# State-space stage: y gathered by turning h, a step later; GpSimd multiplies quarters by C; the residual is added on TensorE; ScalarE's small work in a new order

## The chip, the cores and the metric

One core of a Trainium2 chip runs the whole kernel. The metric is device time in microseconds, the median of several runs. A core has five engines with instruction queues of their own that run in order: TensorE (PE in the profile; its weight loads are PEld), VectorE (DVE), ScalarE (ACT), GpSimd (POOL) and SyncE (SP, here only DMA issues). They wait for each other by semaphores.

## The reference, cut to what matters

A state-space layer of width 512 with 16 states on 2 sequences of 2048 tokens, then attention, then a mixture of experts. Only the first is touched:

```
xz = norm(x) @ W_in.T;  x_ssm, z = split(xz)
xc = silu(causal_conv4(x_ssm) + conv_b)
dt_raw, B, C = split(xc @ W_x.T)                      # 1, 16, 16 columns
dt = softplus(dt_raw * dt_w + dt_b)
h[t, d, n] = exp(dt * A[d, n]) * h[t-1, d, n] + dt * xc * B[t, n]
y[t, d]    = sum_n h[t, d, n] * C[t, n] + xc * D
x1 = x + (y * silu(z)) @ W_out.T
```

## The kernel before, in words

The stage cuts the tokens into chunks of 512 (CH), 4 in each of 2 sequences, and goes through them in turn, c = 2i + b, 8 chunks. Channels lie on the partitions: 512 channels are KI = 4 "quarters" of 128. A chunk is 16 steps, one for each state n. In a step:

- GpSimd makes bx = u * B_n, 128x2048 (L391), up to four steps ahead (ring of 4). The row of B comes by a broadcast DMA (`load_b`, L271).
- ScalarE makes dA = exp(dt * A), one 128x512 quarter at a time (L606), into two PSUM banks. A quarter can be written when the scan two quarters back is over.
- VectorE scans four quarters (L767) into h[n % 4]. Between the second and the third it multiplies the state of the step before by C (L774, 128x2048), where C_n was spread over the partitions by TensorE (`spread_c`, L652) into the single bank `c_ps`.
- ScalarE copies the last column of each scan into `state` (L499) before that multiplication.
- TensorE adds h*C into y_ps (4 banks, channels on the partitions) by a product with the identity (`collect`, L673, four products, eight records). At step n it does first `side`, then waits for the multiplication of state n - 1, spreads C_n, and collects n - 1. The scans of step n wait for the collect of n - 4.

The work of neighbouring chunks is hidden in these steps: `side` on TensorE, `side` and `between` on ScalarE (`between` stands ahead of the exponential of quarter 2, `side` after that of quarter 3), and the `if n == ...` lines on GpSimd. It is the input projection (L626), convolution (L634), the rows of dt, B and C (L642, L648), softplus (L475 to L495), the normalisation of the chunk after next (GpSimd, L343), silu of xc and z, and the output projection of the chunk before (L659), whose result VectorE adds to the residual (L758). The gate y * silu(z) is on VectorE in step 1 (L781). All of TensorE's small products go through one PSUM bank, `fill`, which is handed back and forth by the counts `s_full` and `s_free`. The order of its users is written out by hand as `fill_T`, `fill_E` and so on.

`prologue` does the first chunk's work and most of the second's ahead of the first scan; after the last scan come the gate, the output projection and the store of the last chunk.

The loop that couples ScalarE to VectorE:

```python
for d in range(KI):
    m = ND * c + KI * n + d
    if d == 2:
        if n > 0 or has_prev:
            save_state(*((c, b, n - 1) if n > 0 else (c - 1, 1 - b, NS - 1)))
        between(i, b, n, has_next)
    wait(act, s_scan, m - 1)
    nc.scalar.activation(dA[:, d % 2, :], dt[:, b, d, :], ACT.Exp, ...).then_inc(s_da, 1)
side(i, b, n, has_next)
```

## Time and profile before

| | |
|---|---|
| median of 3 runs | 3388.3 us (3386.0 to 3394.4) |
| profiled execution, its own time | 3382.5 us |
| its span, first to last instruction | 3381.1 us |
| mean granted TensorE clock | 0.934 of full |
| busy over the whole span | PE 2905.4, DVE 2411.4, ACT 1905.4, POOL 1090.3 us |
| broadcast of a row of B (L271), issue to landing | 3.1 us median of 128 |
| state-space stage: first scan / last store issued | 112.5 / 1081.0 us |

The page gives totals over stages with different limits, so the stage is read from queries with a window. "Timeline" lists instructions in order of time, neighbours of one line merged with their count; in brackets stands the idle time before them and who ended it. "Groups" are all instructions of one line and form. "Waits" sum the idle time of an engine by the instruction that waited and the one that released it. TensorE's fp32 product of 512 columns shows as two records.

### The profile page before, as it was taken

The numbers are of one execution on the slowest core, as the hardware profiler recorded it, in microseconds if no ns is written. First come the engines' busy times: TensorE is split into PE (matmuls) and PEld (weight loads), VectorE is DVE, ScalarE is ACT, GpSimd is POOL, SyncE is SP. The second block draws the span as 40 slices with busy tenths as digits, with TensorE's granted clock in tenths as the row PEclk, the third lists the DMA queues.
The fourth block names the chain that finished last, engine by engine and source line by source line (L and its number), as shares of the span: only waits on it lengthen the run. The fifth ranks groups of instructions, "written<-read, shape, count | busy, mean of one in ns | idle before, by whom it ended". The sixth has DMA issues, their size and how long they took to land. (4 is left out here: it accounts for less than half of the span.)

```text
span 3381.1 us, 45342 instructions
## 1 busy us (share of the span) xinstructions
PE 2905.4 (86%) x12880; PEld 1119.3 (33%) x12881; DVE 2411.4 (71%) x2674; ACT 1905.4 (56%) x3514; POOL 1090.3 (32%) x652
## 2 busy tenths in 40 slices
PE   5798899889775949999999999999999872999990
PEld 1234334334332512222222222222222262666650
DVE  0699999999996758888888888888888273111113
ACT  3556655665542517777777777777777611222320
POOL 2889778878862530000000000000000045000006
PEclk8999999999998969999999999999999975999995
DMA  1111111111111531111111111111110045111114
GB/s 42 41 50 48 41 57 55 39 48 49 41 48 39 183 94 32 38 39 39 39 39 39 38 34 36 37 39 39 39 39 10 30 144 201 46 45 45 45 37 146
DMA packets 123093, 185.25 MB, mean 55 GB/s; under 512 B 30224, under 2 KB 77968, under 8 KB 122896
## 3 DMA queue, kind: packets, MB, share of 16 engines
q1 hardware_dynamic: 109072, 142.95, 14.9%
q0 software_dynamic: 13824, 39.86, 3.7%
q8 instruction: 101, 1.65, 0.2%
q14 instruction: 96, 0.79, 0.1%
HBM read 138.01 MB, written 44.43 MB: 54 GB/s over the span
## 5 line engine op out<-in xcount | busy, mean ns | idle before, releaser
L1514 DVE TENSOR_REDUCE nmh<-ring 128x2 f32<-128x1024 f32 x1024 | 1188.0, 1218 | 226.5 <-PE ring L1406 225.1
L1387 ACT ACTIVATE prob<-s_ps 128x512 f32<-128x512 f32 x2048 | 1058.6, 605 | 315.9 <-PE s_ps L1427 313.7
L767 DVE TENSOR_TENSOR_SCAN h<-dA,state,bx 128x512 f32<-128x512 f32 x512 | 618.6, 1268 | 116.1 <-ACT dA L606 115.5
L391 POOL TENSOR_TENSOR bx<-u,bb 128x2048 f32<-128x2048 f32 x128 | 578.9, 4527 | 194.1 <-DVE h L767 193.9
L1427 PE MATMUL s_ps<-qs,ks 98*128 98x512 bf16 x2048 | 598.9, 388 | 16.9 <-issue 13.5
L1439 PE MATMUL acc<-prob,vst 128*32 128x512 f32 x4096 | 550.2, 609 | 0.7 <-ACT prob L1387 0.7
L606 ACT ACTIVATE dA<-dt,aneg 128x512 f32<-128x512 f32 x512 | 348.9, 691 | 270.4 <-DVE h L767 270.3
L673 PE MATMUL y_ps<-h,ident 128*128 128x512 f32 x1024 | 482.6, 616 | 1.1 <-DVE h L774 1.1
L1406 PE MATMUL ring<-k,q 64*128 64x512 bf16 x2048 | 368.4, 396 | 43.4 <-DMA k<-parts 23.6
L1427 PEld LDWEIGHTS s_ps<-qs,ks 98*128 98x128 bf16 x2048 | 157.6, 97 | 516.5 <-ACT prob L1387 423.1
L774 DVE TENSOR_TENSOR h<-h,c_ps 128x2048 f32<-128x2048 f32 x128 | 290.2, 2267 | 4.5 <-PE c_ps L652 4.2
L2225 DVE TENSOR_TENSOR mid<-sl,c_ps 128x512 f32<-128x512 f32 x72 | 49.5, 688 | 325.3 <-ACT sl L2210 325.3
L673 PEld LDWEIGHTS y_ps<-h,ident 128*128 128x128 f32 x1024 | 204.0, 199 | 226.6 <-issue 218.8
L1329 POOL CAST nmr<-a_rowf 16x128 bf16<-16x128 f32 x32 | 8.9, 279 | 769.9 <-ACT a_rowf L1372 769.9
L1406 PEld LDWEIGHTS ring<-k,q 64*128 64x128 bf16 x2048 | 79.7, 94 | 483.5 <-DVE nmh L1514 273.8
L1339 POOL TENSOR_TENSOR att<-oraw,rec 128x256 f32 (+1 forms) x32 | 19.8, 619 | 634.0 <-DVE rec L1528 634.0
L626 PE MATMUL fill<-xT,w_in 128*128 128x512 f32 x256 | 131.9, 640 | 38.0 <-ACT zs L446 18.4
L2210 ACT ACTIVATE sl<-a_ps 128x512 f32<-128x512 f32 x72 | 43.0, 597 | 208.0 <-PE c_ps L2274 208.0
L2166 POOL DMA_DIRECT2D xt<-slots_in x72 | 38.8, 539 | 355.7 <-PE x_ps L2238 348.8
L2274 PE MATMUL a_ps<-w,m_xT 128*128 x288 | 137.4, 600 | 0.3 <-issue 0.3
L2259 PE MATMUL o_ps<-w,midT 128*128 x576 | 136.4, 380 | 0.8 <-ACT midT L2206 0.8
L2274 PE MATMUL c_ps<-w,m_xT 128*128 x288 | 135.7, 594 | 0.0
(221 smaller groups left out, 2563.8 us busy)
## 6 DMA issues: line engine op xcount, KB each, us to landing
bb<-b_rows SPq DMA_DIRECT2D x128, 256.0 KB, 3.1
q<-parts SPq DMA_DIRECT2D x256, 64.0 KB, 2.1
parts<-part POOLq DMA_DIRECT2D x48, 256.0 KB, 3.1
qs<-parts SPq DMA_DIRECT2D x192, 64.0 KB, 2.8
ks<-parts SPq DMA_DIRECT2D x192, 64.0 KB, 2.8
xt<-slots_in POOLq DMA_DIRECT2D x72, 128.0 KB, 2.3
slots_out<-yt SPq DMA_DIRECT2D x72, 128.0 KB, 1.7
k<-parts SPq DMA_DIRECT2D x256, 32.0 KB, 2.0
```

The costliest lines, as they stand in the source:

```text
L391: nc.gpsimd.tensor_tensor(bx[:, n % BR], u[:, b], bb[:, n % RB, None, :].to_broadcast([P, KI, CH]), ALU.mult).then_inc(s_bx, 1)
L606: nc.scalar.activation(dA[:, d % 2, :], dt[:, b, d, :], ACT.Exp, scale=aneg[:, d, n:n + 1]).then_inc(s_da, 1)
L673: last = nc.tensor.matmul(y_ps[:, d, :], ident[:, :], h[:, n % HR, d, :], start=False, stop=(n == NS - 1))
L767: nc.vector.tensor_tensor_scan(h[:, n % HR, d, :], dA[:, d % 2, :], bx[:, n % BR, d, :], state[:, b, n, d:d + 1], ALU.mult, ALU.add).then_ ...
L774: nc.vector.tensor_tensor(h[:, n % HR], h[:, n % HR], c_ps[:, None, :].to_broadcast([P, KI, CH]), ALU.mult).then_inc(s_hc, 1)
L1387: nc.scalar.activation(prob[:, k % PR, j, :], s_ps[:, tile % SR, :], ACT.Exp, scale=SC).then_inc(s_exp, 1)
L1406: ins = nc.tensor.matmul(ring[:, s, half, :], q4[r, slot, t * P:(t + 1) * P], k4[r, slot, s * CH:(s + 1) * CH], start=True, stop=True)
L1427: nc.tensor.matmul(s_ps[:, tile % SR, :], ks[:, par, hh, t * P:(t + 1) * P], qs[:, par, hh, j * CH:(j + 1) * CH], start=True, stop=True).t ...
L1439: last = nc.tensor.matmul(acc[32 * j:32 * j + 32, :], vst[:, par, t, v0:v0 + 32], prob[:, k % PR, j, :], start=(t == 0), stop=(t == KT - 1))
L1514: nc.vector.tensor_reduce(nmh[:, slot, t, 2 * s:2 * s + 2], ring[:, s, :, :], AX.X, ALU.max, negate=True).then_inc(s_free[s], 1)
L2259: last = nc.tensor.matmul(o_ps[:, q % 2, 0:DM], midT[:, q % 2, m, :], of_expert(w2, e_down, m), start=(m == 0), stop=(m == KF - 1))
L2274: last = nc.tensor.matmul(dst[:, q % 2, :], xT[:, q % 2, k, :], of_expert(w, e_up, k), start=(k == 0), stop=(k == KM - 1))
```

## The change

- **Turned y.** y_ps and zs now hold tokens on the partitions and channels along the bank. `collect` turns 16 blocks of 128x128 with TensorE's transpose (`is_transpose`) that adds to PSUM, and does so one step later (n - 2 instead of n - 1). z is projected in the same layout (`project_z`). The skip part is 16 products of 128 columns instead of 4 of 512, and stands in step 2 behind `spread_c`. After the gate the result is turned back (`gated`, 4 blocks for each quarter, copied by ScalarE in `take_g`), then projected.
- **Quarters by GpSimd.** For 8 of the 16 states (SHARED) VectorE multiplies three quarters by C and GpSimd the fourth, four steps later, with rows of C that come by DMA (`c_rows`, `load_c`, two buffers). `collect` waits for it before its last four turnings.
- **Residual.** TensorE adds x by a product with the identity in `project_out`; ScalarE copies the result out (`take_o`) instead of VectorE's addition.
- **Normalisation** goes from GpSimd to ScalarE (`normalize`, four instructions), with a small product on VectorE (`mean_part`).
- **Order.** ScalarE's small work has new places: softplus_in one quarter at a time, take_conv 3 in step 0, take_rows in step 2, z in steps 9 and 10, the chunk after next from step 11. TensorE's side work moves with it. VectorE's gate goes from the middle to the end of step 1.
- At the end the turning back uses four free banks (`end_banks`), each copied by ScalarE, and store_x1 moves from step 13 to 15.

```diff
+    RC = 2
+    SHARED = (0, 2, 10, 11, 12, 13, 14, 15)
+    NP = len(SHARED)
...
+        zs = sb("zs", [P, 2, TT, DI])
...
+        y_ps = ps("y_ps", [P, TT, DI])
...
+            def load_c(i, b, n):
+                c, k = 2 * i + b, SHARED.index(n)
+                wait_apart(sp, s_prst, 32 * (c + 1), s_w)
+                wait_apart(sp, s_hp, NP * c + k - RC + 1, s_w)
+                sp.dma_start(cc[:, k % RC, :], c_dram[b, n:n + 1, :].partition_broadcast(P)
+                             ).then_inc(s_c[k % RC], 16)
...
+                    if n - RC in SHARED:
+                        load_c(i, b, n - RC)
+                    elif n - RC + NS in SHARED and has_prev:
+                        load_c(*prv(i, b), n - RC + NS)
...
+            def times_c(c, n):
+                k = SHARED.index(n)
+                wait(pool, s_c[k % RC], 16 * ((NP // RC) * c + k // RC + 1))
+                wait(pool, s_sv, NS * c + n + 1)
+                nc.gpsimd.tensor_tensor(h[:, n % HR, KI - 1, :], h[:, n % HR, KI - 1, :], cc[:, k % RC, :], ALU.mult
+                                        ).then_inc(s_hp, 1)
...
+                    if n - BR in SHARED:
+                        times_c(c, n - BR)
+                    elif n - BR + NS in SHARED and has_prev:
+                        times_c(c - 1, n - BR + NS)
                     if n == 6 and has_next:
                         rest(c + 1, 1 - b)
-                    if n == 8 and has_two(i):
-                        norm_apply(c + 2)
-                    if n == 9 and has_next:
-                        rest_of_rest(c + 1)
                     if n == 10 and has_next:
                         rounding(c + 1)
                     if n == 11 and has_next:
+                        rest_of_rest(c + 1)
                         log_part(c + 1, 1 - b)
...
+            def normalize(c, t):
+                wait(act, s_mr, c + 1)
+                last = nc.scalar.activation(xn[:, t, :], xn[:, t, :], ACT.Identity, bias=mr[:, t:t + 1],
+                                            scale=rs[:, t:t + 1])
+                if t == TT - 1:
+                    last.then_inc(s_xn, 1)
...
+            def between(i, b, n, has_prev, has_next):
                 c = 2 * i + b
                 two = has_two(i)
-                if n == 1 and has_next:
-                    take_conv(c + 1, 1 - b, 3)
-                if n == 3 and has_next:
-                    take_rows(c + 1, 1 - b)
-                if n == 8 and has_next:
-                    take_z(c + 1, 1 - b, 1)
-                if n == 9 and has_next:
-                    take_z(c + 1, 1 - b, 3)
+                if has_next:
+                    if n in (3, 4):
+                        softplus_in(c + 1, 1 - b, 2 * n - 6)
+                    if n == 8:
+                        second_part(c + 1, 1 - b)
+                    if n in (9, 10):
+                        take_z(c + 1, 1 - b, 2 * n - 18)
+                if n in (6, 7) and has_prev:
+                    take_g(c - 1, 1 - b, 2 * n - 11)
                 if two:
-                    if n == 10:
-                        take_xT(c + 2, 1)
+                    if n in (6, 7):
+                        normalize(c + 2, n - 6)
+                    if n == 9:
+                        normalize(c + 2, 2)
+                        normalize(c + 2, 3)
                     if n == 11:
-                        take_conv_in(c + 2, 1)
+                        take_xT(c + 2, 0)
                     if n == 12:
-                        take_conv_in(c + 2, 3)
-                    if n in (13, 14, 15):
-                        take_conv(c + 2, b, n - 13)
-
-            def side(i, b, n, has_next):
+                        place_halo(c + 2, b)
+                    if n in (12, 13):
+                        take_conv_in(c + 2, 2 * n - 24)
+                    if n == 14:
+                        take_conv(c + 2, b, 0)
+
+            def side(i, b, n, has_prev, has_next):
                 c = 2 * i + b
                 two = has_two(i)
+                if n == 0 and has_next:
+                    take_conv(c + 1, 1 - b, 3)
                 if n == 1:
                     if has_next:
                         silu_xc(c + 1, 1 - b)
                     silu_z(c, b)
                     power_tables()
-                if n == 2 and two:
-                    root(c + 2)
-                if n == 3 and has_next:
-                    softplus_in(c + 1, 1 - b, 0)
-                if n == 4 and has_next:
-                    softplus_in(c + 1, 1 - b, 1)
-                if n == 5 and has_next:
-                    softplus_exp(c + 1)
-                if n == 6 and has_next:
-                    softplus_plus(c + 1)
-                    second_part(c + 1, 1 - b)
-                if n == 7 and has_next:
-                    softplus_minus(c + 1)
-                    take_z(c + 1, 1 - b, 0)
-                if n == 8 and has_next:
-                    softplus_ln(c + 1, 1 - b)
-                    take_z(c + 1, 1 - b, 2)
-                if n == 9:
+                if n == 2:
                     if has_next:
+                        take_rows(c + 1, 1 - b)
+                    if two:
+                        root(c + 2)
+                if n in (5, 6) and has_prev:
+                    take_g(c - 1, 1 - b, 2 * n - 10)
+                if n in (7, 8) and has_prev:
+                    take_o(c - 1, n - 7)
+                if has_next:
+                    if n in (3, 4):
+                        softplus_in(c + 1, 1 - b, 2 * n - 5)
+                    if n == 5:
+                        softplus_exp(c + 1)
+                    if n == 6:
+                        softplus_plus(c + 1)
+                    if n == 7:
+                        softplus_minus(c + 1)
+                    if n == 8:
+                        softplus_ln(c + 1, 1 - b)
+                    if n in (9, 10):
+                        take_z(c + 1, 1 - b, 2 * n - 17)
+                    if n == 14:
                         third_part(c + 1, 1 - b)
-                    if two:
-                        take_xT(c + 2, 0)
                 if two:
-                    if n == 10:
-                        place_halo(c + 2, b)
-                        take_conv_in(c + 2, 0)
                     if n == 11:
-                        take_conv_in(c + 2, 2)
+                        take_xT(c + 2, 1)
+                    if n in (12, 13):
+                        take_conv_in(c + 2, 2 * n - 23)
+                    if n in (14, 15):
+                        take_conv(c + 2, b, n - 13)
...
+            def project_z(c, t):
+                wait(pe, s_free, fill_Z(c, t))
+                for k in range(KM):
+                    last = nc.tensor.matmul(fill[:, :], xT[:, k, t * P:(t + 1) * P], w_in[:, k, DI:2 * DI],
+                                            start=(k == 0), stop=(k == KM - 1))
+                last.then_inc(s_full, 1)
+
+            def turn_back(bank, b, d):
+                for t in range(TT):
+                    last = nc.tensor.transpose(bank[:, t * P:(t + 1) * P], zs[:, b, t, d * P:(d + 1) * P], ident[:, :])
+                return last
+
+            def gated(c, b, d):
...
             def project_out(c, b, half):
                 wait(pe, s_free, fill_O(c, half))
+                wait(pe, s_xr, 16 * (c + 1))
                 for t in (2 * half, 2 * half + 1):
+                    nc.tensor.matmul(fill[:, (t % 2) * DM:(t % 2 + 1) * DM], ident[:, :], xres[:, t, :],
+                                     start=True, stop=False)
                     for d in range(KI):
                         last = nc.tensor.matmul(fill[:, (t % 2) * DM:(t % 2 + 1) * DM],
-                                                zs[:, b, d, t * P:(t + 1) * P], w_out[:, d, :],
-                                                start=(d == 0), stop=(d == KI - 1))
+                                                zs[:, b, t, d * P:(d + 1) * P], w_out[:, d, :],
+                                                start=False, stop=(d == KI - 1))
                 last.then_inc(s_full, 1)
             def skip_part(c, b):
                 wait(pe, s_g, c)
+                for t in range(TT):
+                    for d in range(KI):
...
                 for d in range(KI):
-                    last = nc.tensor.matmul(y_ps[:, d, :], diag[:, d, :], xc[:, b, d, :],
-                                            start=True, stop=False)
-                last.then_inc(s_dx, 1)
-
-            def collect(n):
-                for d in range(KI):
-                    last = nc.tensor.matmul(y_ps[:, d, :], ident[:, :], h[:, n % HR, d, :],
-                                            start=False, stop=(n == NS - 1))
+                    if n in SHARED and d == KI - 1:
+                        wait(pe, s_hp, NP * c + SHARED.index(n) + 1)
+                    for t in range(TT):
+                        last = nc.tensor.matmul(y_ps[:, t, d * P:(d + 1) * P], h[:, n % HR, d, t * P:(t + 1) * P],
+                                                ident[:, :], is_transpose=True, start=False,
+                                                stop=(n == NS - 1 and d == KI - 1))
                 last.then_inc(s_ys, 1)
             def prologue():
...
                 two = has_two(i)
-                if n == 0 and has_next:
-                    convolve(c + 1, 3)
-                if n == 1:
-                    skip_part(c, b)
-                if n == 2 and has_next:
-                    project_rows(c + 1, 1 - b)
-                if n == 3 and has_next:
-                    spread_dt(c + 1)
-                if n in (5, 6) and has_prev:
-                    project_out(c - 1, 1 - b, n - 5)
-                if n in (7, 8) and has_next:
-                    project_in(c + 1, KI + 2 * n - 14)
-                    project_in(c + 1, KI + 2 * n - 13)
+                if has_next:
+                    if n == 0:
+                        convolve(c + 1, 3)
+                    if n == 2:
+                        project_rows(c + 1, 1 - b)
+                    if n == 3:
+                        spread_dt(c + 1)
+                if has_prev:
+                    if n in (5, 6):
+                        gated(c - 1, 1 - b, 2 * n - 10)
+                        gated(c - 1, 1 - b, 2 * n - 9)
+                    if n in (7, 8):
+                        project_out(c - 1, 1 - b, n - 7)
+                if has_next:
+                    if n == 8:
+                        project_z(c + 1, 0)
+                    if n == 9:
+                        project_z(c + 1, 1)
+                        project_z(c + 1, 2)
+                    if n == 10:
+                        project_z(c + 1, 3)
                 if two:
-                    if n == 9:
-                        transposes(c + 2, 0)
-                        transposes(c + 2, 1)
                     if n in (10, 11):
-                        project_in(c + 2, 2 * n - 20)
-                        project_in(c + 2, 2 * n - 19)
-                    if n in (12, 13, 14):
-                        convolve(c + 2, n - 12)
+                        transposes(c + 2, n - 10)
+                    if n == 11:
+                        project_in(c + 2, 0)
+                    if n == 12:
+                        project_in(c + 2, 1)
+                        project_in(c + 2, 2)
+                    if n == 13:
+                        project_in(c + 2, 3)
+                        convolve(c + 2, 0)
+                    if n in (14, 15):
+                        convolve(c + 2, n - 13)
             def chunk(i, b, has_prev, has_next):
                 c = 2 * i + b
...
-                        collect(NS - 1)
+                        collect(c - 1, n - 2 + NS)
             every_chunk(pe, prologue, chunk)
+            collect(NC - 1, NS - 2)
             wait(pe, s_hc, NS * NC)
-            collect(NS - 1)
...
-                                        c_ps[:, None, :].to_broadcast([P, KI, CH]), ALU.mult
+                mine = KI - 1 if n in SHARED else KI
+                nc.vector.tensor_tensor(h[:, n % HR, 0:mine], h[:, n % HR, 0:mine],
+                                        c_ps[:, None, :].to_broadcast([P, mine, CH]), ALU.mult
                                         ).then_inc(s_hc, 1)
...
-                    if n == 1 and has_prev:
-                        gate(c - 1, 1 - b)
                     if n > 0:
                         times_c(c, b, n - 1)
                     elif has_prev:
                         times_c(c - 1, 1 - b, NS - 1)
-                    if n in (6, 7) and has_prev:
-                        residual(c - 1, n - 6)
                     scans(c, b, n, 1)
                     if n == 1 and has_two(i):
                         norm_stats(c + 2)
+                    if n == 1 and has_prev:
+                        gate(c - 1, 1 - b)
+                    if n == 4 and has_two(i):
+                        mean_part(c + 2)
             every_chunk(dve, prologue, chunk)
             times_c(NC - 1, 1, NS - 1)
             gate(NC - 1, 1)
```

## Rows read from the trace of the kernel before

**Rows 1.** Windows, 500 to 600 us: length, PE, PEld, DVE, ACT, POOL, clock, DMA.
```profile
500.00:600.00 100.00, 90.14 (x224) 41.75 (x225) 96.74 (x71) 60.73 (x97) 84.09 (x23) 0.95 0.18 54
```

**Rows 2.** Groups by form, first 1300 us: count, busy us, mean ns, idle before.
```profile
L767 DVE TENSOR_TENSOR_SCAN h<-dA,state,bx 128x512 f32<-128x512 f32 x512 | 618.6, 1268 | 116.1 <-ACT dA L606 115.5 <-issue 0.6
L391 POOL TENSOR_TENSOR bx<-u,bb 128x2048 f32<-128x2048 f32 x128 | 578.9, 4527 | 194.1 <-DVE h L767 193.9
...
L774 DVE TENSOR_TENSOR h<-h,c_ps 128x2048 f32<-128x2048 f32 x128 | 290.2, 2267 | 4.5 <-PE c_ps L652 4.2 <-ACT state L499 0.3
...
L758 DVE TENSOR_TENSOR xres<-fill,xres 128x512 f32<-128x512 f32 x16 | 11.0, 690 | 9.5 <-PE fill L659 9.5
...
L1004 ACT COPY v_all<-v_ps 128x256 f32<-128x256 f32 x8 | 2.4, 387 | 0.1
```

**Rows 3.** Waits, first 1300 us: us in total, times, longest.
```profile
DVE h L767 <- ACT dA L606: 115.5, 27, 91.3
```

**Rows 4.** The scans' line by itself: min, median, max ns, first and last start.
```profile
L767 DVE TENSOR_TENSOR_SCAN h<-dA,state,bx x512: 1248/1265/1296, 112.5 to 1060.2; 128x512 f32<-128x512 f32 x171
```

**Rows 5.** Timeline of VectorE: start us, length us, what, count, idle before.
```profile
527.89 2.46 DVE L767 TENSOR_TENSOR_SCAN h<-dA,state,bx 128x512 f32<-128x512 f32 x2 [0.93 <-ACT dA L606]
...
547.37 4.80 DVE L767 TENSOR_TENSOR_SCAN h<-dA,state,bx 128x512 f32<-128x512 f32 x4
552.08 2.27 DVE L774 TENSOR_TENSOR h<-h,c_ps 128x2048 f32<-128x2048 f32 x1
554.26 2.45 DVE L767 TENSOR_TENSOR_SCAN h<-dA,state,bx 128x512 f32<-128x512 f32 x2
```

**Rows 6.** Timeline of ScalarE, same columns.
```profile
494.67 0.78 ACT L475 ACTIVATE xs<-fill,dtb,dtw 128x512 f32<-128x512 f32 x1 [1.09 <-PE fill L648]
...
496.01 0.78 ACT L475 ACTIVATE xs<-fill,dtb,dtw 128x512 f32<-128x512 f32 x1
...
522.48 1.99 ACT L492 ACTIVATE tB<-tB,minus 128x2048 f32<-128x2048 f32 x1
...
549.85 0.69 ACT L606 ACTIVATE dA<-dt,aneg 128x512 f32<-128x512 f32 x1 [0.48 <-DVE h L767]
...
550.81 0.59 ACT L434 COPY xs<-fill 128x512 f32<-128x512 f32 x1 [0.15 <-PE fill L626]
```

**Rows 7.** Timeline of TensorE's products in the stage.
```profile
493.51 1.12 PE L648 MATMUL fill<-pr,sel_f 17*128 17x512 f32 x2
...
509.14 3.62 PE L659 MATMUL fill<-w_out,zs 128*128 128x256 f32 x16
...
550.61 0.38 PE L652 MATMUL c_ps<-c_parts,sel 96*128 96x512 bf16 x1
550.83 3.60 PE L673 MATMUL y_ps<-h,ident 128*128 128x512 f32 x8
554.27 1.88 PE L626 MATMUL fill<-xT,w_in 128*128 128x512 f32 x4
...
562.30 3.60 PE L634 MATMUL fill<-xs,taps 128*128 128x512 f32 x8
```

**Rows 8.** Timeline of TensorE in the routing stage and the expert stage.
```profile
2709.57 1.95 PE L1889 MATMUL g_ps<-gate,gT 128*128 128x8 f32 x16 [1.36 <-ACT gT L1827]
...
2713.63 5.21 PE L1863 MATMUL h_ps<-wo,attT 128*128 128x256 f32 x16 [1.18 <-ACT attT L1815]
...
2902.40 0.60 PE L2266 MATMUL m_ps<-m_ident,mid 128*128 128x128 f32 x4
```

**Rows 9.** Timeline of TensorE, a skip part and a collect after idling.
```profile
237.80 5.40 PE L667 MATMUL y_ps<-xc,diag 128*128 128x512 f32 x8 [2.38 <-DVE zs L781]
...
263.44 0.61 PE L652 MATMUL c_ps<-c_parts,sel 96*128 96x512 bf16 x1 [4.12 <-DVE h L774]
263.84 6.33 PE L673 MATMUL y_ps<-h,ident 128*128 128x512 f32 x8
```

**Rows 10.** Timeline of GpSimd, the rounding.
```profile
524.59 4.16 POOL L358 TENSOR_TENSOR tB<-tB,xs 128x2048 f32<-128x2048 f32 x1
```

141 lines of the change are left out of this document (86 added, 55 removed).

## The prediction

> **What bounds the kernel now.** I read the page's 40 slices first: the state-space stage fills the first third of the span and is the only stage that the diff touches. Then the busy time of one hundred-microsecond stretch [rows 1]: VectorE 96.7, TensorE 90.1, GpSimd 84.1, ScalarE 60.7. VectorE leads, and its groups say with what [rows 2]: 512 scans and 128 multiplications by C. The waits [rows 3] tell how full it is: of 115.5 us of idling before scans, 91.3 is the one wait for the prologue, so only 24.2 us is lost after it. The scans run from 112.5 to 1060.2 plus one scan [rows 4], 949 us; 925 of them are work. So a microsecond less of VectorE work is a microsecond gained, as long as nobody else makes it wait.
>
> The timeline of VectorE gives a step [rows 5]: two scans, a multiplication, two scans; four scans are 4.71 (547.37 to 552.08), the multiplication 2.18 to the next start, a step 6.89. ScalarE is coupled to it through two dA banks [rows 6]. I set a step's clock to zero at its first scan. The exponential of quarter 1 runs from 0.1 to 0.8, then the state copy and whatever stands in `between`, from 0.83 on; then quarter 2; quarter 3 when scan 1 is over, 2.45 to 3.1; then whatever stands in `side`; the next step's quarter 0 must be ready at 6.89. So `between` must be over near 3.9 and `side` near 6.2. All of today's 24 us is ScalarE overrunning such a slot, as 0.93 in [rows 5].
>
> **VectorE's work.** A quarter of the multiplication: (2267 - 690) ns over 1536 elements is 1.03 ns an element [rows 2], 0.53 us for 512. 64 of 128 multiplications lose a quarter, 63 of them before the last scan: -33.2. A shortened step is 6.36. Residual: 14 of 16 lie before the last scan, 0.69 less the 0.09 by which neighbours overlap: -8.4. Six small `mean_part`, not in the trace, below 0.3 each and not below zero: +0.9 taken. The gate only moves. Sum -40.7.
>
> **GpSimd's work.** Eight products of 128x512, a quarter of 4.53 each [rows 2], +9.1 a chunk; normalisation -4.8. It has slack: 84 of 100 busy. All scans take 1248 to 1296 ns [rows 4] with GpSimd busy beside most of them, so I add nothing for the pair; 0 to 3 us as a bound.
>
> **SyncE's queue.** Eight more broadcast loads a chunk, as large as those of B, and a second store of rows. `load_c` waits for the product two before it and `load_b` stands behind it; but that wait ends right after bx n, and the load behind is for bx n + 4, some 20 us of GpSimd work on, where a load lands in half a step. Nothing added; if it did bind, GpSimd would come late in steps 14 to 2, where it has 5 us in hand.
>
> **TensorE's work.** [rows 7]: spreading C takes 0.22 to the next start, collecting 3.43, a projection 1.7 (ScalarE may read 1.91 after its start), a convolution 3.43 (3.63), half an output projection 3.5, dt 0.86 (1.16). A turning takes one record where a product takes two: four last 0.60 with 0.27 of it tail [rows 8], so 0.11 each, and a collect of sixteen is 1.75: -1.7 a step, if a turning that accumulates costs as much. Bounds 1.75 to 3.5 (two records each). The skip part becomes 32 records of 128 columns, each with a new weight load; 16 records of 8 columns with new weights take 1.95 [rows 8], under 0.12 each, so 3.5 to 3.9, about as now. Output projection: 20 records of 0.215 for 16, 4.3, ready 4.5. So TensorE gets lighter by about a fifth. It isn't the bound, though: what matters is when its results arrive, because ScalarE's queue is in order, and dA stands behind each wait.
>
> **Walking the new order, step by step.** A wait in ScalarE's `between` or `side` holds the dA queued behind it, and VectorE's scan behind that.
> - Step 3. In step 2 TensorE waits for multiplication 1 (ends 4.63), spreads C (0.22), then does the skip part (3.5), then collects (1.75): 10.2, which is 3.3 in step 3. Only then comes the dt row, ready at 4.4. ScalarE stands before it since 0.83, now in `between`, with quarter 2 behind. The Abs/Relu pair is 1.34 [rows 6], dA 0.62: 6.4, where the scan wants it at 4.0 (2.36 + 1.65). 2.4 lost, and the second pair in `side` 0.3 more: 2.7, in 7 chunks, 18.9. Today the wait is 1.09 in `side` and costs 0.67.
> - Step 7. The output projection can start when ScalarE has taken the last turned bank, 1.45, and is ready at 6.0. ScalarE, at `side` since 3.1, waits, copies (0.58), does the minus-one pass (1.9 in [rows 6]), then dA: 9.2 against 6.89, 2.3 lost in 6 chunks. In the last chunk, without that pass, 0.4.
> - Steps 12 to 14. GpSimd's rounding needs that late pass (8.6), a lag of over 3 on [rows 10], where it starts right after bx. Four more large operations of 4.2 to 4.5 stand among its bx, so the product for state 10, behind bx 14, is ready 46.5 after step 7's start. TensorE collects state 10 at step 12 and waits for it until 4.4 in step 13. Behind it stand a projection, ready 6.3 (wanted near 5.1: 1.2 lost), a convolution, C for step 13 (late, hidden), and in step 14 the convolution that ScalarE waits for until 8.4: 3.5 lost. 4.7 in each of 5 chunks, 2.2 in the first, which has no step-7 stall ahead: 25.7.
> - Elsewhere the slots hold: step 1's 6.5 us of silu and tables lies beside 1.86 of statistics and the gate, steps 9 to 12 have waits of 0.3 with room. +2 for these.
>
> **The clock.** After an idle of 4.12 the collect took 6.33, not 3.60; after 2.38 the skip part took 5.40, though its eight records are of the same size [rows 7, 9]. In the new order TensorE is idle for some 7 us into step 4, then has only turnings until step 7. So I let half of the output projection of step 7 run at 1.2 GHz: +2.3 in 7 chunks, 16, and a third of the 1.8 that the skip part lost there, +0.6 in 7, 4. Bounds: 0 and +4.3 for each output projection, 0 and 5.5 for each step 3.
>
> **What a page says against it.** In the routing stage, turnings and 8-column products fill much of the time, idles are only 1.2 to 1.4, and yet the product of 16 records takes 5.21 [rows 8] where 3.5 is the full-clock time [rows 7]: turnings seem to hold the clock poorly. The Trainium skill, "TensorE: Matmul & The Clock Gate", section "Part 4: PE-mode transpose", states that transposes do not count as busy for the clock gate in the way matmuls do. By that rule the third rival is what happens; without it the sum stands.
>
> **Ends.** Prologue: normalising goes from GpSimd to ScalarE, whose chain leads to the first scan: twice four of 0.39 [rows 2], +3.2, the GpSimd time saved hangs on nothing. Epilogue: four turned banks and their copies (about 3), 8 records more (2), less a quarter product and half a collect: +3.
>
> **Sum.** Idle within the stage 18.9 + 13.8 + 0.4 + 25.7 + 2 + 20 = 80.8 less today's 24.2: +56.6. Work -40.7. Ends +6.2. Total +22; against the profiled execution (span 3381.1, its own time 3382.5) 3404, and the median of the runs lies 5.8 above that execution: 3410.
>
> **Rivals.** (1) *The slots hold.* The stage still waits only about 24 us, because the dt row and the output projection are early enough: -40.7 + 6 = -35, 3353; with half the stalls walked, -7 to -18, 3370 to 3381. For it: VectorE is the fullest engine, TensorE gets lighter. Against: TensorE's order in steps 2 and 3. (2) *About equal*: the work saved and the stalls cancel within 10 us; that is the walk without the clock term, +2, 3390. (3) *The clock falls for good.* If turnings don't hold it, steps 9 to 12 run at 1.2 GHz too. Their products and turnings, 19 us at 2.4, become 38 in 27 us of steps: +11 in 6 chunks, 66, with the other terms 3470. It decides from the point where doubled work passes a step, 3.4 at full clock; steps 9 and 12 have 5.4. (4) *Accumulating turnings take two records*: 1.75 more a step, no relief; behind the late products of 12 to 14 this adds 3 to 4 a chunk, 3435.
>
> **Chances.** Forecast (stalls win, 3399 to 3430) 0.37; rival 1 0.28; rival 2 0.19; rival 3 0.11; rival 4 0.05. Over 0.3% faster, which is about what a measurement can tell: rival 1, 0.28; same 0.19; slower 0.53. The range reaches into rival 1 and up to the weaker forms of 3: 3352 to 3450; the likeliest case's own is 3399 to 3430.
>
> **What would show it.** Right: VectorE's idle before scans behind dA near 70 to 80 us after the first wait, the longest before quarter 2 of step 3 and quarter 0 of steps 8 and 15; ScalarE's waits for `fill` by the dt row and the output projection; TensorE waiting for GpSimd's h in step 12; collects of 1.75 to 3.5. The three-quarter multiplication at 1.74. Wrong: dt taken without a wait in step 3, a lighter TensorE that is early everywhere, or a clock that stays at 2.4 GHz through step 7.

## The result, and the profile after

| | before | after |
|---|---|---|
| median (8 runs each) | 3387.2 us (3382.4 to 3394.5) | 3401.15 us (3391.7 to 3407.0) |
| ratio of the medians, 95% interval | | 1.0040 (1.0028 to 1.0052) |
| profiled execution, its own time / its span | 3382.5 / 3381.1 us | 3403.2 / 3402.5 us |
| mean granted TensorE clock | 0.934 | 0.905 |
| first / last scan starts | 112.5 / 1060.2 us | 122.1 / 1075.1 us |

The changed kernel is 0.4% slower, 14 us by the medians, 21.4 by the two spans. The window of 500 to 600 us answers to [rows 1], columns as there:

```profile
500.00:600.00 100.00, 75.72 (x374) 53.72 (x373) 89.06 (x68) 63.77 (x109) 79.96 (x23) 0.91 0.17 56
```

VectorE had 96.7 us of work in it and now has 89.1; TensorE went from 90.1 to 75.7, though it issues more records. Work was taken away, and the time was not used. The groups by form, first 1300 us, answer to [rows 2]:

```profile
L875 DVE TENSOR_TENSOR_SCAN h<-dA,state,bx 128x512 f32<-128x512 f32 x512 | 618.8, 1263 | 112.4 <-ACT dA L668 111.7
...
L763 PE MATMUL y_ps<-ident,h 128*128 128x128 f32 x2048 | 314.6, 319 | 19.6 <-POOL h L398 19.6
...
L883 DVE TENSOR_TENSOR h<-h,c_ps 128x2048 f32<-128x2048 f32 x64 | 144.6, 2260 | 0.0
...
L883 DVE TENSOR_TENSOR h<-h,c_ps 128x1536 f32<-128x1536 f32 x64 | 110.7, 1730 | 6.2 <-PE c_ps L735 5.9 <-ACT state L546 0.3
L398 POOL TENSOR_TENSOR h<-h,cc 128x512 f32<-128x512 f32 x64 | 80.9, 1263 | 16.1 <-ACT state L546 16.1
```

64 multiplications now take 1.73 us instead of 2.26. The idle time before the scans is 111.7 us, nearly as before [rows 2, 3], but its make-up isn't: the first wait, for the prologue, is now 46.2, because an operation of VectorE in the prologue splits it, and what is left is 65.5 where it was 24.2.

The 21.4 us of the spans lie as follows. First scan 9.6 later. From the first to the last scan 953.0 instead of 947.7, +5.3. From the last scan to the issue of the last store 21.9 instead of 20.8, +1.1. From there to the end +5.4, in stages that are the same in both kernels. The +5.3 of the scans' stretch is the sum that matters. VectorE is busy for 877.0 us of it where it was busy for 917.5 before, so its work is 40.5 less and its idle time 45.9 more (76.0 against 30.1). Of the 76.0, 74.8 are waits on other engines: 65.5 for dA, 5.9 for c_ps, 3.1 for y_ps in two gates, 0.3 for the state.

### The profile page after: what moved, and what is told of

Same layout as the page of the kernel before. It is cut to its first block and busy times, and to the rows that moved or that the text cites. A ratio compares the mean times of both kernels' runs of the same rounds, so it can differ in the third digit from the quotient of the medians.

```text
span 3402.5 us, 48600 instructions
## 1 busy us (share of the span) xinstructions
PE 2797.3 (82%) x14288; PEld 1253.4 (37%) x14289; DVE 2370.1 (70%) x2666; ACT 1944.1 (57%) x3594; POOL 1131.7 (33%) x684
## 5 line engine op out<-in xcount | busy, mean ns | idle before, releaser
L875 DVE TENSOR_TENSOR_SCAN h<-dA,state,bx 128x512 f32<-128x512 f32 x512 | 618.8, 1263 | 112.4 <-ACT dA L668 111.7
L1515 PE MATMUL ring<-k,q 64*128 64x512 bf16 x2048 | 368.0, 396 | 43.6 <-DMA k<-parts 23.9
L763 PE MATMUL y_ps<-ident,h 128*128 128x128 f32 x2048 | 314.6, 319 | 19.6 <-POOL h L398 19.6
L763 PEld LDWEIGHTS y_ps<-ident,h 128*128 128x128 f32 x2048 | 296.8, 168 | 51.3 <-POOL h L398 22.9
L883 DVE TENSOR_TENSOR h<-h,c_ps 128x1536 f32<-128x1536 f32 (+1 forms) x128 | 255.3, 1995 | 6.2 <-PE c_ps L735 5.9
L735 PE MATMUL c_ps<-c_parts,sel 96*128 96x512 bf16 x128 | 58.8, 459 | 163.5 <-DVE h L883 163.1
```

The lines of the kernel that those rows point to most:

```text
L763: last = nc.tensor.matmul(y_ps[:, t, d * P:(d + 1) * P], h[:, n % HR, d, t * P:(t + 1) * P], ident[:, :], is_transpose=True, start=False, ...
L875: nc.vector.tensor_tensor_scan(h[:, n % HR, d, :], dA[:, d % 2, :], bx[:, n % BR, d, :], state[:, b, n, d:d + 1], ALU.mult, ALU.add).then_ ...
L883: nc.vector.tensor_tensor(h[:, n % HR, 0:mine], h[:, n % HR, 0:mine], c_ps[:, None, :].to_broadcast([P, mine, CH]), ALU.mult).then_inc(s_h ...
L1515: ins = nc.tensor.matmul(ring[:, s, half, :], q4[r, slot, t * P:(t + 1) * P], k4[r, slot, s * CH:(s + 1) * CH], start=True, stop=True)
```

## Where VectorE waits: one chunk of the kernel after

Three timelines of the chunk whose step 2 begins at 867, columns as in [rows 5]. VectorE, steps 2 to 4 and the end of step 7:

```profile
876.49 1.73 DVE L883 TENSOR_TENSOR h<-h,c_ps 128x1536 f32<-128x1536 f32 x1
880.77 2.46 DVE L875 TENSOR_TENSOR_SCAN h<-dA,state,bx 128x512 f32<-128x512 f32 x2 [2.55 <-ACT dA L668]
883.43 2.46 DVE L875 TENSOR_TENSOR_SCAN h<-dA,state,bx 128x512 f32<-128x512 f32 x2 [0.20 <-ACT dA L668]
...
913.43 2.46 DVE L875 TENSOR_TENSOR_SCAN h<-dA,state,bx 128x512 f32<-128x512 f32 x2 [2.30 <-ACT dA L668]
```

ScalarE in the same stretch:

```profile
878.71 0.78 ACT L522 ACTIVATE xs<-fill,dtb,dtw 128x512 f32<-128x512 f32 x1 [3.64 <-PE fill L731]
879.39 0.77 ACT L524 ACTIVATE dt<-fill,dtb,dtw 128x512 f32<-128x512 f32 x1
880.05 1.30 ACT L668 ACTIVATE dA<-dt,aneg 128x512 f32<-128x512 f32 x2
...
910.23 0.59 ACT L461 COPY xres<-fill 128x512 f32<-128x512 f32 x1 [2.92 <-PE fill L745]
910.71 2.01 ACT L539 ACTIVATE tB<-tB,minus 128x2048 f32<-128x2048 f32 x1
912.62 1.29 ACT L668 ACTIVATE dA<-dt,aneg 128x512 f32<-128x512 f32 x2
```

And TensorE:

```profile
871.91 0.39 PE L735 MATMUL c_ps<-c_parts,sel 96*128 96x512 bf16 x1 [2.45 <-DVE h L883]
872.14 3.74 PE L754 MATMUL y_ps<-diag,xc 128*128 128x128 f32 x32
875.71 1.91 PE L763 MATMUL y_ps<-ident,h 128*128 128x128 f32 x16
877.55 1.12 PE L731 MATMUL fill<-pr,sel_f 17*128 17x512 f32 x2
...
906.14 1.89 PE L745 MATMUL fill<-w_out,zs 128*128 128x256 f32 x8
907.87 0.59 PE L742 MATMUL fill<-xres,ident 128*128 128x256 f32 x2
908.30 1.89 PE L745 MATMUL fill<-w_out,zs 128*128 128x256 f32 x8
```

Read backwards: the scan at 880.77 waits 2.55 for an exponential at 880.05. That one stands behind the Abs/Relu pair at 878.71, which had waited 3.64 for the dt row at 877.55. And the dt row stands behind C, the skip part and a collect. In step 7 the same shape: the exponentials at 912.62 stand behind a pass of 2.01, that behind a copy that waited 2.92 for the output projection.

## The experiments

Each kernel was timed in rounds with the kernel before beside it. There are three groups of runs: e1 to e4 ("before" 3375.2 us), c1, e5, e6 and e7 (3376.5), e8 to e10 (3377.1, on another chip). A ratio is to the runs of "before" in the same group, and differs by up to 0.0011 from the quotient of the medians; its interval is 95%. On these chips the kernel before is some 10 us faster than in the table of the result, so medians are compared within this table alone. "Stretch" is the time from the start of the first scan to the start of the last, from the profile.

| kernel | median us | ratio | stretch | idle before scans for dA, first wait left out |
|---|---|---|---|---|
| c1_after | 3393.9 | 1.0050 (1.0037 to 1.0064) | 949.0 | 61.5 |
| e1_dt_early | 3372.0 | 0.9983 (0.9974 to 0.9992) | 935.8 | 41.0 |
| e2_minus_first | 3384.1 | 1.0019 (1.0008 to 1.0030) | 938.5 | 55.4 |
| e3_both | 3360.2 | 0.9948 (0.9934 to 0.9962) | 919.0 | 27.7 |
| e4_both_pool | 3351.2 | 0.9918 (0.9903 to 0.9932) | 919.5 | 28.1 |
| e5_twice | 3458.8 | 1.0238 (1.0223 to 1.0253) | 1018.4 | 124.0 |
| e6_ordinary | 3457.2 | 1.0234 (1.0219 to 1.0249) | 1018.1 | 123.8 |
| e7_noshare | 3399.3 | 1.0070 (1.0057 to 1.0083) | 958.8 | 45.4 |
| e8_mended | 3342.9 | 0.9896 (0.9882 to 0.9911) | 910.7 | 29.7 |
| e9_share10 | 3334.1 | 0.9876 (0.9862 to 0.9890) | 900.3 | 28.7 |
| e10_mended_noshare | 3356.2 | 0.9939 (0.9927 to 0.9951) | 924.9 | 13.7 |

**c1_after: the change itself, once more, beside the others.**

> The changed kernel itself, as the yardstick for the other three on this chip: 1.004 of the kernel before, first scan between 115 and 122 us depending on where TensorE's clock rises in the prologue.

1.0050 against 1.0040: the two agree within their intervals. Its scans began at 115.0, 7.1 us earlier than in the profile of after, and its stretch is 4.0 shorter: 1.3 us over the 947.7 of before, with 41.9 more idle and 40.6 less work. So VectorE gave back all of its saved work in both profiles, and 1 to 5 us more. That is also how far two profiles of the same code lie apart.

### Step 3: the dt row behind C, the skip part and a collect

**e1_dt_early** moves the two products of the dt row into step 2, behind `spread_c` and ahead of the skip part:

```diff
-                    if n == 3:
-                        spread_dt(c + 1)
...
+                        if has_next:
+                            spread_dt(c + 1)
                         skip_part(c, b)
```

> The changed kernel with one move: TensorE spreads the dt row in step 2, right behind spread_c, ahead of the skip part and the collect, instead of at the head of step 3. Theory A (the order of TensorE's queue makes the step-3 stall): VectorE's idle before the scan of quarter 2 in step 3, 26 us in 7 chunks in the changed kernel, goes to under 3; the rest stays; about 3401 - 22 = 3379. Rival B (the dt row is late because ScalarE's take_rows or the clock is late): the stall stays above 12 us and the time above 3390. Rival C (ScalarE is full anyway, the stall comes back in step 4 or 5): idle moves there, time within 5 us of the changed kernel.

22 us less than c1_after. The waits before scans in its stage:

```profile
DVE h L875 <- ACT dA L668: 82.0, 23, 41.0
...
DVE h L875 <- PE y_ps L763: 9.5, 6, 1.7
```

The idle for dA fell by 20.5 us and no scan of step 3 waits for it. But a new wait of 9.5 us came: with step 3 short, the scans of step 4 catch up with the collect that has to free their place in h, 1.4 to 1.7 us in each of six chunks. So the cause is shown, and the stall had covered a second one behind it. The stretch shows 13 us of the gain; the medians show 22, and where the other 9 lie the profiles don't say (the profiled execution of c1_after is 9.8 us below its median, that of e1 4.9).

### Steps 7 and 13 to 15: the minus-one pass behind the output projection

**e2_minus_first** puts `take_o(c - 1, 0)` behind the pass instead of ahead of it:

```diff
-                if n in (7, 8) and has_prev:
+                if n == 8 and has_prev:
                     take_o(c - 1, n - 7)
...
                     if n == 7:
                         softplus_minus(c + 1)
+                if n == 7 and has_prev:
+                    take_o(c - 1, 0)
```

> The changed kernel with one move: in ScalarE's step 7 the minus-one pass of softplus stands ahead of the copy of the output projection, not behind it. Both theories: VectorE's idle before step 8, 2.2 us in 6 chunks, goes to about 0.3 (-11), and GpSimd's wait for the pass before the rounding (23.9 us in 7) to about 0. Theory A (GpSimd's lag from that wait makes the stalls of steps 13 and 14): these fall from 4.6 to about 2.2 us a chunk, TensorE's wait for GpSimd's h in step 12 goes, and the time falls by 20 to 24, to 3379. Rival B (TensorE's own chain of projections and convolutions makes them): they stay at 4.6, the time falls by 11, to 3390.

9.8 us less than c1_after. By the time that is rival B's figure; the waits show that theory A's chain is there too. Step 7's wait shrank, and part of it came back one step later. The second scan here is the one that opens step 9:

```profile
890.48 2.46 DVE L878 TENSOR_TENSOR_SCAN h<-dA,state,bx 128x512 f32<-128x512 f32 x2 [0.41 <-ACT dA L671]
...
898.56 2.46 DVE L878 TENSOR_TENSOR_SCAN h<-dA,state,bx 128x512 f32<-128x512 f32 x2 [1.08 <-ACT dA L671]
```

ScalarE shows the same shape as in step 7, with the next pass of softplus behind the copy of the second half of the output projection:

```profile
895.45 0.59 ACT L461 COPY xres<-fill 128x512 f32<-128x512 f32 x1 [1.79 <-PE fill L748]
895.94 1.92 ACT L542 ACTIVATE u<-xs 128x2048 f32<-128x2048 f32 x1
```

GpSimd's wait for the pass fell from 23.9 us to 3.0 (seven times each), TensorE's wait for GpSimd's quarter from 18.5 in eleven times (c1_after) to 1.5 in three. The idle of steps 13 to 15 fell from about 4.5 to 1.95 us in three of the six chunks. The first, which has no output projection in step 7, stayed at 3.4, one stayed at 6.5, and one fell to 3.9. That it fell at all, though nothing was changed there, shows the chain: late pass, late rounding, late quarter, late collect, late projection, late dA. Against c1_after steps 7 and 8 idle 5 us less, steps 13 to 15 8 less, and step 3 idles 3 more, since the skip part took 4.86 and 5.01 in two chunks where c1_after has 3.74.

**e3_both** makes both edits.

> Both moves, dt row early and minus-one pass first. If the two stalls are independent the gains add: -42 to -46 against the changed kernel, 3357, which is 30 below the kernel before; VectorE's idle behind dA in the stage, 65 us in the changed kernel, near 20. If GpSimd or ScalarE becomes the bound once VectorE no longer waits, the sum is 10 us or more short of the two single gains.

33.7 us less than c1_after; the two alone give 21.9 and 9.8. The gains add, and more than add in the stretch (30.0, where the two alone give 13.2 and 10.5). It is short of the 42 to 46 expected because the second edit alone brought half of what had been expected of it. With two small products moved and one line put behind another the change is 0.5% faster than the kernel before.

**e4_both_pool** is e3_both with the prologue's two normalisations back on GpSimd (four `tensor_scalar` on `xn` for each of the first two chunks, as the kernel before does it):

```diff
+            def norm_apply(c):
+                wait_apart(pool, s_rs, c + 1, s_w)
+                for t in range(TT):
+                    last = nc.gpsimd.tensor_scalar(xn[:, t, :], xn[:, t, :], mv[:, t, 0:1], rs[:, t:t + 1],
+                                                   ALU.subtract, ALU.mult)
+                last.then_inc(s_xn, 1)
...
-                for t in range(TT):
-                    normalize(0, t)
...
-                for t in range(TT):
-                    normalize(1, t)
```

> As the last one, and in the prologue alone the two normalisations are again on GpSimd, as in the kernel before. The first scan came at 112.5 us before and at 122.1 after. Theory A (four ScalarE passes each time, and a stretch at 1.2 GHz that they lengthen): it comes at 112.5 to 114 again and the time falls by 8 to 10 more, to 3348. Rival B (the clock's phase at the start made half of it): only 4 to 5 come back.

9 us less by the medians. Its profiled execution, 3355.9 us, shows a part of it. Its first transpositions began at 13.05 instead of 15.38 in e3_both, and the projection ahead of which the second normalisation stood waits 5.97 instead of 7.93: 4.3 us gained by the move. But three projections more ran at 1.2 GHz there (3.78 us each, not 1.98), and two other products took 1.4 longer, so that the scans began at 117.6 against 115.1. The other 5 us of the medians this profile doesn't place.

### Do turnings hold TensorE's clock?

The pair **e5_twice** and **e6_ordinary** gives `collect` 32 records of the same size in both, once as turnings, once as ordinary products of two records each. e5 counts every h*C twice in y.

```diff
-                    for t in range(TT):
...
+                    for r in range(2):
+                        for t in range(TT):
+                            last = nc.tensor.matmul(y_ps[:, t, d * P:(d + 1) * P],
+                                                    h[:, n % HR, d, t * P:(t + 1) * P],
+                                                    ident[:, :], is_transpose=True, start=False,
+                                                    stop=(n == NS - 1 and d == KI - 1 and r == 1))
```

```diff
-                                                ident[:, :], is_transpose=True, start=False,
+                                                ident[:, :], start=False,
```

> The changed kernel, but collect turns each block twice (32 turnings instead of 16), so that y counts double: a test of the clock. In the last eight steps, where TensorE has nothing else, a step holds 3.7 us of turnings in 6.4 to 6.9 us, as much as the kernel before had of products, whose collects there took 3.6 us at 2.4 GHz. If turnings hold the clock as products do, those collects of 32 take 3.6 us, the granted clock of that stretch is over 0.9. If they don't (the rule of the page), they take near 7 us and the clock stays under 0.7. Time: 1.75 us more in each step behind which ScalarE waits: plus 20 to 60 us.

> The changed kernel, but collect uses ordinary products with the identity in place of the turnings, the block of h as weights: 32 records of 128 columns. Same columns and weight loads as with doubled turnings. The clock in the last eight steps: over 0.9 if products of 128 columns count fully, and then the difference to the doubled turnings is the kind of instruction; the collects take 3.6 to 3.9 us. Time: 1.8 us more in each collect, as with doubled turnings if the clock is the same; less if only products hold it.

In the last eight steps of the last chunk TensorE has only C to spread and h to collect. These windows there (c1_after, e5, e6; length, then busy us and records of PE, PEld, DVE, ACT, POOL, then the clock, the DMA share and GB/s):

```profile
1016.00:1064.00 48.00, 26.96 (x131) 23.18 (x130) 48.00 (x37) 20.78 (x36) 25.28 (x10) 0.68 0.21 61
```

```profile
1094.00:1142.00 48.00, 31.68 (x248) 29.17 (x247) 46.71 (x37) 20.80 (x37) 24.42 (x10) 0.94 0.18 57
```

```profile
1092.00:1140.00 48.00, 32.38 (x250) 30.50 (x249) 46.89 (x37) 20.59 (x36) 24.36 (x9) 0.96 0.21 61
```

With 32 turnings the granted clock was 0.94, with 32 ordinary records 0.96, with 16 turnings 0.68. One collect of each, at full clock:

```profile
1133.17 3.66 PE L764 MATMUL y_ps<-ident,h 128*128 128x128 f32 x32
```

```profile
1132.47 3.74 PE L763 MATMUL y_ps<-ident,h 128*128 128x128 f32 x32
```

So in these windows a turning costs the engine what an ordinary record of the size does and keeps the clock as well. The clock of the changed kernel is lower there because its collect is half as long, not because it turns. The rule of the Trainium skill that the prediction weighed ("TensorE: Matmul & The Clock Gate", "Part 4: PE-mode transpose") is not borne out by these windows. The two kernels also price what the turning saves: both are 63 to 65 us slower than c1_after, with 62 us more idle before scans. That is more than the 20 to 60 expected of e5. So in this order of work the halved collect is worth more than VectorE's 41 us of saved work: ScalarE waits for what stands behind it.

### What GpSimd's share is worth

**e7_noshare** leaves every multiplication whole on VectorE, **e10_mended_noshare** does it in the mended kernel below:

```diff
-    SHARED = (0, 2, 10, 11, 12, 13, 14, 15)
+    SHARED = ()
```

> The changed kernel without GpSimd's share: SHARED is empty, VectorE multiplies all four quarters in all 16 states. VectorE's work rises by 64 times 0.53 = 34 us. Theory A (the share is worth what it takes from VectorE): plus 25 to 34 us, less what TensorE's wait for GpSimd's h in step 12 cost, so about plus 25. Rival B (the share brings nothing, since VectorE only waits longer for dA): under plus 12. TensorE's waits for h from GpSimd vanish, and with them, if GpSimd's lag is what makes steps 13 and 14 late, about half of the stalls there.

Only 5.4 us slower than c1_after, though VectorE has 34 us more to do. The waits of VectorE:

```profile
DVE h L875 <- ACT dA L668: 91.7, 26, 46.3
DVE zs L890 <- PE y_ps L763: 6.6, 3, 3.7
```

The wait for c_ps is gone, steps 13 to 15 idle 0.7 to 1.8 us a chunk instead of 4.5, and step 3 idles 2.0 to 3.9 instead of 2.6 to 5.4. In the change as it stands, the share brings 5 of its 34 us by the medians and 10 by the stretch, which is rival B. Two things went at once, though: the longer multiplication gives TensorE and ScalarE time to catch up, and TensorE no longer waits for GpSimd's late quarter. This run doesn't separate them.

### A version that beats both

**e8_mended** is e4_both_pool with four more moves: the skip part goes into step 2's `side`, behind `project_rows` and so ahead of the wait for the multiplication; `second_part` goes from step 8 to 10 and GpSimd's `rest_of_rest` from 11 to 12; the first convolution of the chunk after next goes behind C of step 13, and ScalarE's second `take_conv` from step 14's `side` to step 15's `between`.

```diff
-                        rest_of_rest(c + 1)
                         log_part(c + 1, 1 - b)
                     if n == 12 and has_next:
+                        rest_of_rest(c + 1)
...
-                    if n == 8:
+                    if n == 10:
                         second_part(c + 1, 1 - b)
...
-                    if n == 14:
-                        take_conv(c + 2, b, 0)
+                    if n in (14, 15):
+                        take_conv(c + 2, b, n - 14)
...
+                if n == 2:
+                    skip_part(c, b)
...
-                        convolve(c + 2, 0)
...
-                        skip_part(c, b)
+                    if n == 13 and has_two(i):
+                        convolve(c + 2, 0)
```

> The fourth experiment's kernel (dt row early, minus-one pass first, prologue normalised on GpSimd) with four more moves against the stalls that its trace still shows: second_part from step 8 to 10 (1.08 us before step 8's quarter 2, 6 chunks), the skip part right behind the rows' projection in step 2, ahead of spread_c (1.1 to 1.4 us before step 4's first scan, 6 chunks), the convolution of step 13 behind spread_c (0.62 to 0.96, 6 chunks), and take_conv 1 from step 14's side to step 15's between (2.3, 6 chunks). If the stalls are each a place in a queue, VectorE's idle behind dA after the first wait falls from 28 to under 12 us and the rest with it: 25 to 30 less, 0.983 to 0.985 of the kernel before. If ScalarE or TensorE is by now full, new stalls take their place and it gains under 12.

8.2 us less than e4_both_pool by the medians of two chips, 8.8 by the stretch. That is the other case of the expectation: the waits for y_ps in step 4 and for c_ps (10.8 us) are gone, but the idle for dA didn't fall, and steps 14 and 15 still lose about 2.1 in five chunks and 5.6 in one:

```profile
DVE h L885 <- ACT dA L676: 70.6, 29, 40.9
```

The wait of 1.08 is still there in six chunks, and the timeline says why. It isn't before quarter 2 of step 8, where `second_part` stood and where the expectation put it, but before the first scan of step 9. Ahead of that stands `side` of step 8: the copy of the output projection's second half, which waits 1.79 for TensorE, and then the pass of 1.91. This is the stall of step 7 once more; putting the pass ahead of the copy there too wasn't tried. And TensorE now waits more for GpSimd's quarter, where e4_both_pool had 1.8 us in two times:

```profile
PE y_ps L771 <- POOL h L405: 8.7, 8, 1.6
```

**e9_share10** gives GpSimd ten quarters instead of eight.

```diff
-    SHARED = (0, 2, 10, 11, 12, 13, 14, 15)
+    SHARED = (0, 1, 2, 3, 10, 11, 12, 13, 14, 15)
```

> The last kernel with ten shared states instead of eight (1 and 3 added, whose products fall into steps where GpSimd idles). VectorE's work falls by 16 times 0.53 = 8.4 us. If the slots hold: 6 to 8 less. If shorter steps only bring new waits for dA (the rule of the unshared run): no gain, plus or minus 3.

8.8 us less again: 16 multiplications lose 0.53 each, 8.5. All of it arrives, since the idle before scans doesn't grow. So shorter steps alone don't bring waits where, as in steps 2 and 4, the engines behind have room:

```profile
DVE h L885 <- ACT dA L676: 70.8, 29, 42.1
```

At 3334.1 us this is the fastest, 1.2% under the kernel before.

> The mended kernel without GpSimd's share (SHARED empty). In the changed kernel as it stands the share brought only 5 to 7 us of the 34 that it takes from VectorE. Theory: it was given back as stalls in steps 12 to 14, so with these mended it is worth 25 to 34: this kernel is slower than the mended one by that much, near the level 0.992 of the kernel before. Rival: the share costs as much as it takes whatever the order, and this kernel is within 12 us of the mended one.

13.3 us slower than e8_mended, of 34 that VectorE has more to do. Its wait line is

```profile
DVE h L885 <- ACT dA L676: 52.8, 16, 39.1
```

13.7 us after the first wait, where e8_mended idles 29.7. So even there 16 us of the share are given back behind dA, and by the medians 21. The measured 13.3 lies between theory (25 to 34) and rival (within 12), nearer to the rival: the share isn't nearly free once the two stalls are gone. Nearly all the waits that e8_mended has and this kernel hasn't are those of the last two steps of a chunk. There TensorE works with hardly a gap from GpSimd's late quarter on (step 13) to the convolution that ScalarE waits for. As in e7, the runs don't say how much of it is the late quarter and how much the shorter steps.

## Point by point

**The mechanism was right:** less work on VectorE, and all of it or a little more given back by ScalarE waiting in order. **That the total fits so well is luck.** The sum was +22 and the spans say +21.4. But the stretch, which the prediction had at +16, grew by 5.3 (1.3 in c1_after), and the ends and the stages behind, which it had at +6, brought 16: 5 of it is the clock in the prologue, and 5 lies in the stages behind, which the change doesn't touch. The prediction's idle term was 11 too high: 5 in the new kernel's idle time, and 6 because it took off only today's waits for dA (24.2), where VectorE idled 30.1 in all. By the prediction's steps, in the profile of after:

| term | predicted | measured |
|---|---|---|
| VectorE's work | -40.7 | -40.5 |
| step 3 | 18.9, and 4 by the clock | 26.0 in 7 chunks |
| step 7 | 13.8 + 0.4, and 16 by the clock | 13.4 + 0.4 |
| steps 12 to 15 | 25.7 | 25.9 |
| elsewhere | 2 | 9.1 |
| all idle after the first wait | 80.8 | 74.8 |
| prologue | +3.2 | +9.6: 4.6 by the code, 5.0 by the clock (c1_after: +2.5) |
| epilogue | +3 | +1.1 |
| stages behind | 0 | +5.4 (c1_after: -6.9) |

**Step 3.** The waits are 4.4, 5.4, 2.6, 4.2, 2.6, 4.2 and 2.8 us; the walk gave 2.7, and the small ones are that. The larger ones are the clock. The prediction had 0.6 a chunk for it here, 4 in all, and it was 7: in four of the seven chunks the skip part took 5.36 to 6.17, where its 32 records take 3.74 at full clock. Here is one of them, the first four records left out:

```profile
504.80 4.92 PE L754 MATMUL y_ps<-diag,xc 128*128 128x128 f32 x28
509.55 1.91 PE L763 MATMUL y_ps<-ident,h 128*128 128x128 f32 x16
```

**Step 7.** 2.20 to 2.30 in six chunks where 2.3 was walked. The +2.3 a chunk for the clock is the term that failed, 16 us. It had been argued from the idle in step 4, and the idle came:

```profile
888.12 0.61 PE L735 MATMUL c_ps<-c_parts,sel 96*128 96x512 bf16 x1 [7.38 <-DVE h L883]
888.52 3.62 PE L763 MATMUL y_ps<-ident,h 128*128 128x128 f32 x16
```

The collect of step 4 ran at 1.2 GHz (3.62, not 1.91) and the next two partly so, 2.94 in step 6. But by 906 the clock was back: eight records of the output projection took 1.89. The slow collects cost nothing, since nobody waits for them. What the prediction lacked was a row that says how soon the clock returns; it took a half where the rows of before gave only bounds, and the bound of 0 was the true one.

**Steps 12 to 15.** The total was right. Its parts were not quite: 3.4 in the first chunk (2.2 predicted), and in the others 4.5 (4.7): 1.2 for the projection (1.2 predicted), then 1.0 for C, which the prediction had called hidden, then 2.3 to 2.4 for the convolution (3.5 predicted). The multiplication waits for C because the step's convolution stands ahead of C on TensorE. One chunk in each view:

```profile
712.32 2.46 DVE L875 TENSOR_TENSOR_SCAN h<-dA,state,bx 128x512 f32<-128x512 f32 x2 [1.21 <-ACT dA L668]
715.77 1.75 DVE L883 TENSOR_TENSOR h<-h,c_ps 128x1536 f32<-128x1536 f32 x1 [0.99 <-PE c_ps L735]
...
722.19 2.46 DVE L875 TENSOR_TENSOR_SCAN h<-dA,state,bx 128x512 f32<-128x512 f32 x2 [2.30 <-ACT dA L668]
```

```profile
708.69 0.66 PE L763 MATMUL y_ps<-ident,h 128*128 128x128 f32 x4 [1.49 <-POOL h L398]
```

**Elsewhere.** 3.1 for the gate's y_ps in two chunks, 2.3 in the first chunk's step 2 (2.1 there before too), and 3.4 in one chunk whose convolution came late. None was walked.

**Prologue.** Both normalisations stand in the chain to the first scan. The first lets the first transpositions begin at 15.21 instead of 12.63, +2.6. The second stands ahead of a copy for which the second projection of z waits, +2.0; here the kernel before, then after:

```profile
73.25 3.78 PE L626 MATMUL fill<-xT,w_in 128*128 128x512 f32 x4 [5.98 <-ACT zs L446]
```

```profile
79.46 3.78 PE L700 MATMUL fill<-w_in,xT 128*128 128x512 f32 x4 [7.94 <-ACT zs L487]
```

So the code costs 4.6 where 3.2 was predicted: four normalisations take 2.06 to 2.08, not four times the 0.39 of a plain copy. The other 5.0 of the 9.6 are the clock's: seven projections of the prologue took 3.58 to 3.78 where before four did, and 1.98 is the full-clock time. The same code in c1_after had three, and its first scan came at 115.0, 7.1 earlier. Here is the second projection of after and of c1_after:

```profile
23.34 3.78 PE L693 MATMUL fill<-xT,w_in 128*128 128x512 f32 x4 [0.68 <-ACT xs L475]
```

```profile
23.20 1.98 PE L693 MATMUL fill<-xT,w_in 128*128 128x512 f32 x4 [0.68 <-ACT xs L475]
```

**GpSimd.** A quarter took 1.263 us, not the 1.13 of a quarter of 4.53. With 64 of them it is 8.4 us more. The scans beside it took 1249 to 1283 ns, the range of before [rows 4].

**Stages behind.** The +5.4 wasn't predicted, and the profiles don't show it to be the change's. From the issue of the last store to the end it is 2305.5 us in after and 2300.1 before, but 2293.2 in c1_after, which is the same code as after. By the medians the change costs 14 us (17 in c1_after's group); the stretch and the two ends, without the clock in the prologue, come to 7 to 11 of them.

**The rivals.** Rival 1, that the slots hold, failed as argued, at step 3 and step 7; but e1, e2 and e3 show how near it was, 34 us for moving two lines. Rival 2, the walk without the clock term, was right in leaving out the clock of step 7: the stretch grew by 5.3, and by 1.3 in c1_after, between the 16 of the forecast and its -4, and rather nearer to it. What lifts the stretch above its -4 is the clock in step 3 and what was not walked, 7 us each, less the waits besides dA that the kernel before had too. Rival 3 would have needed a clock that turnings don't hold; e5 and e6 exclude that, and in the chunk shown the projections of steps 8 and 9 took 1.98, the full-clock time. The clock did fall, to 0.78 in the window of 900 to 1000 us where it was 0.95, but in collects that had room. Rival 4, turnings of two records each, is excluded by the collect of 16 in 1.91.

**What stays open.** About 5 us of the medians between e3_both and e4_both_pool, and 3 to 10 of those between before and after. How much of what the share gives back is GpSimd's late quarter. Whether the last steps of a chunk can be mended: in e8_mended ScalarE waits 3.52 for a convolution that stands behind a collect, the same shape again, but no run took it away, nor the 1.08 behind step 8.

## To carry to other kernels

Where an in-order engine feeds the bottleneck through a double buffer, price each of its small steps by when its input arrives, not by its length: two products of 1.1 us together, placed behind 5.6 us of others, cost 13 us of the stretch and 22 by the medians. Work taken from the fullest engine shortens the slots of the engines behind it and can make one of them late. Here between three fifths and five sixths of it came back as waits (20.7 and 28.6 of 34), but nothing of the last 8.5, which were taken in steps with room; take the stalls away first, then share where there is room. And a wait that is removed may uncover another, so read the next one before counting the gain, and read from the timeline which operation stands ahead of it: a wait put down to the wrong step cost e8_mended a move that did nothing for it. Last, a single profile's total can fit a sum by chance; go by its parts, and by a second profile of the same code.

## What the hardware showed that was not expected

- A turning that adds to PSUM takes no longer than one that starts a bank: four take 0.66 either way. 16 of 128x128 in 1.91 us, 32 in 3.66, against 3.74 for 32 ordinary records.
- Turnings keep TensorE's clock as ordinary products do: 0.94 against 0.96 in the same eight steps.
- After 7.38 us of idling the clock was at 1.2 GHz for the next collect and partly for two more, and at 2.4 GHz 18 us later, with TensorE working only a part of that time.
- The prologue's first projection ran at 1.2 GHz in every profile, and how many of the others do differs between two profiles of the same code (seven and three in all), which moves the first scan by 7 us.
- GpSimd's product of 128x512 takes 1.263 us, more than a quarter of the 4.53 of 128x2048.
